# Recommender tower on one core: a segment's products and its table lookup issued alternately on TensorE, and ScalarE's copies reordered

## The reference, cut to what matters

```python
e = jnp.stack([tbl_0[ids[:, 0]], ..., tbl_25[ids[:, 25]]], axis=1)
combined = jnp.concatenate((dense_features[:, None, :], e), axis=1)      # 2048 x 27 x 128
interactions = jnp.einsum('bfd,bgd->bfg', combined, combined)
interactions_flat = interactions[:, iu, ju]                              # 351 pairs
h = jnp.concatenate([dense, interactions_flat, dense], axis=1)
h = jnp.maximum(h @ W_top1 + b_top1, 0.0)                                # 512
h = jnp.maximum(h @ W_top2 + b_top2, 0.0)                                # 256
y = h @ W_top3
```

## Time and profile before

| | |
|---|---|
| median of 3 runs | 406.02 us (405.79 to 406.1) |
| the profiled execution's own time | 405.83 us |
| its span, first to last instruction | 404.0 us |
| mean granted TensorE clock | 0.996 |
| TensorE matmul busy | 389.2 us (96%) |
| VectorE, ScalarE, GpSimd busy | 250.6, 221.8, 279.4 us |

### The profile page before, as it was taken

The page is one execution under the profiler, slowest core; times in us unless marked ns, Lnnn a source line. Parts: engine busy times, 40 slices in busy tenths (PEclk is TensorE's granted clock), DMA queues, the critical chain, the costliest instruction groups (busy, mean ns, idle before and its releaser), DMA issues.

```text
span 404.0 us, 8455 instructions
## 1 busy us (share of the span) xinstructions
PE 389.2 (96%) x3264; PEld 376.1 (93%) x3264; DVE 250.6 (62%) x683; ACT 221.8 (55%) x465; POOL 279.4 (69%) x296
## 2 busy tenths in 40 slices
PE   6978879999999999999999999999999999999998
PEld 4867779999999999999999999999999999999896
DVE  5899878568395737749375756739474765913421
ACT  2354177647464555737554664746455673756462
POOL 6777877777777777777777777777777777774000
PEclk9999989999999999999999999999999999999999
DMA  8996234323332332333333233333343222221000
GB/s 185 265 287 161 67 74 97 80 75 82 76 78 78 86 80 73 85 80 78 68 87 80 80 84 77 80 80 74 81 84 80 60 53 60 54 54 40 2 2 0
DMA packets 24596, 33.98 MB, mean 84 GB/s; under 512 B 8590, under 2 KB 18342, under 8 KB 24557
## 3 DMA queue, kind: packets, MB, share of 16 engines
q0 software_dynamic: 9216, 18.89, 19.4%
q1 hardware_dynamic: 13260, 14.41, 14.7%
q10 hardware_dynamic: 2080, 0.15, 0.5%
HBM read 33.41 MB, written 0.01 MB: 83 GB/s over the span
## 4 chain that ended last, share of the span: by engine, by line
PE 91%; DVE 4%; ACT 3%; issue 2%; DVEq 0%
PE look L511 29%; PE prod L541 26%; PE mlp L559 10%; PE turn L522 8%; PE mlp L570 6%; PE mlp L561 3%; PE mlp L506 3%; DVE onehot L400 2%; PE mlp L578 2%; PE prod L585 2%; ACT feats L293 1%; PE mlp L551 1%; ACT diag L308 1%; DVE table_lo L406 1%; PE prod L631 1%
## 5 line engine op out<-in xcount | busy, mean ns | idle before, releaser
L271 POOL DMA_INDIRECT rows<-in_tbl,ids x288 | 278.5, 967 | 89.2 <-issue 85.7
L308 ACT ACTIVATE diag<-prod 27x216 f32<-27x216 f32 x256 | 87.5, 342 | 139.8 <-PE prod L541 131.5
L400 DVE TENSOR_SCALAR onehot<-wanted,row_no 125x256 fp32r<-125x256 int32 x462 | 144.3, 383 | 13.1 <-PE look L511 13.1
L511 PE MATMUL look<-onehot,table_hi 125*128 125x256 f32 x494 | 128.3, 297 | 3.0 <-DVE onehot L400 2.7
L511 PE MATMUL look<-onehot,table_lo 125*128 125x256 f32 x494 | 123.1, 286 | 0.0
L541 PE MATMUL prod<-feats 128*123 128x108 f32 x1024 | 119.8, 270 | 2.2 <-ACT feats L293 2.2
L541 PEld LDWEIGHTS prod<-feats 128*123 128x123 f32 x1024 | 115.3, 188 | 3.2 <-ACT feats L293 3.0
L511 PEld LDWEIGHTS look<-onehot,table_hi 125*128 125x128 f32 x494 | 96.3, 195 | 4.3 <-issue 4.2
L428 DVE TENSOR_SCALAR h<-mlp,b_sb 128x128 f32<-128x128 f32 x86 | 24.9, 345 | 118.3 <-PE mlp L561 73.9
L511 PEld LDWEIGHTS look<-onehot,table_lo 125*128 125x128 f32 x494 | 96.6, 196 | 0.0
L293 ACT ACTIVATE feats<-turn 128x512 f32<-128x512 f32 (+1 forms) x80 | 78.3, 1019 | 1.1
(11 more groups left out here) (52 smaller groups left out, 145.8 us busy)
## 6 DMA issues: line engine op xcount, KB each, us to landing
wanted<-in_small_ids SPq DMA_DIRECT2D x56, 128.0 KB, 3.3
rows<-in_tbl,ids POOLq DMA_INDIRECT x288
feats<-in_tbl SPq DMA_DIRECT2D x7, 448.0 KB
dense<-in_dense_rows SPq DMA_DIRECT2D x16, 64.0 KB, 3.4
w_sb<-in_w_pairs SPq DMA_DIRECT2D x1, 702.0 KB
table<-in_tbl SPq DMA_DIRECT2D x1, 560.0 KB
w_sb<-in_w SPq DMA_DIRECT2D x1, 512.0 KB
feats<-in_tbl SPq DMA_DIRECT2D x7, 52.0 KB
```

What stands on the lines that cost most here:

```text
L271: gp.indirect_dma_start(rows[:, q % SLOTS_OF_ROWS, f * D:(f + 1) * D], None, large_tables[g + f], bass.IndirectOffsetOnAxis(ap=ids[:, t, g ...
L308: last = nc.scalar.activation(diag[t % 2][W * i:W * i + SLOTS, s * SEG_GROUPS * SLOTS:(s + 1) * SEG_GROUPS * SLOTS], prod_part(prod[s % 2] ...
L400: made = nc.vector.tensor_scalar(onehot[v % 2][:, c - row_nos_at(h), :], wants, row_no[:, c:c + 1], None, ALU.is_equal)
L511: last = nc.tensor.matmul(look_bank(v)[:, 0:BS], part_of(part, k)[:, c * D:(c + 1) * D], onehot[v % 2][:, c, :], start=(c == 0 and part is ...
```

## The change

In every segment that has a lookup, TensorE no longer does products and lookup one after the other. The new `products_and_look_up` first makes all waits of both, and then issues one group of the products, the two matmuls of one chunk of the lookup, the next group, and so on. The eighth table's last two chunks come at the end alone. `prod_full` is given by the eighth group, `look_full` by the last lookup matmul. The turned chunks and the tower parts follow behind. On ScalarE `empty_lookup` moves ahead of `empty_turn` and `place_dense`. The segments of tiles 14 and 15, the head and the other engines' orders stay.

```diff
                     if s == 0 and t >= 2:
                         copy_result(t - 2)
+                    if (v := lookup_at(t, s)) is not None:
+                        empty_lookup(v)
                     if t + 1 < TILES:
                         for k in TURNS_AT[s]:
                             empty_turn(t + 1, k)
                         if s == 1:
                             place_dense(t + 1)
-                    if (v := lookup_at(t, s)) is not None:
-                        empty_lookup(v)
...
-                if v >= NS:
-                    pe.wait_ge(look_read, v)
-                elif v >= 2:
+                if v >= 2:
                     pe.wait_ge(look_read, v - 1)
...
+            def products_and_look_up(t, s, v):
+
+                k = v % NS
+                wait_for_products(t, s)
+                if v < 2 * NS:
+                    pe.wait_ge(hi_ready[k], 1)
+                    pe.wait_ge(lo_ready[k], 1)
+                pe.wait_ge(onehot_ready, v + 1)
+                pe.wait_ge(look_read, v)
+                for c in range(CH[k]):
+                    if c < SEG_GROUPS:
+                        last_group = group_products(t, s, c)
+                        if c == SEG_GROUPS - 1:
+                            last_group.then_inc(prod_full, 1)
+                    for part in (table_hi, table_lo):
+                        last = nc.tensor.matmul(look[:, 0:BS], part_of(part, k)[:, c * D:(c + 1) * D],
+                                                onehot[v % 2][:, c, :], start=(c == 0 and part is table_hi),
+                                                stop=(c == CH[k] - 1 and part is table_lo))
+                last.then_inc(look_full, 1)
...
             for t in range(LAST):
                 for s in range(SEGS):
-                    products(t, s)
+                    if (v := lookup_at(t, s)) is not None:
+                        products_and_look_up(t, s, v)
+                    else:
+                        products(t, s)
                     if s == 0 and t >= 2:
                         third_layer(t - 2)
                     if t + 1 < TILES:
                         for k in TURNS_AT[s]:
                             turn_rows(t + 1, k)
-                    if (v := lookup_at(t, s)) is not None:
-                        look_up(v)
```

More of the change, by code:

```diff
@@ L495, in look_up @@
                     pe.wait_ge(raw_in[k], 32)
-                elif v == k or v == NS + k and k in WHOLE_FIRST:
+                else:
                     pe.wait_ge(hi_ready[k], 1)
@@ L524, in turn_rows, with wait_for_products @@
                 last.then_inc(turn_full, 1)
-            def products(t, s):
+            def wait_for_products(t, s):
                 m = SEGS * t + s
@@ L535, in products @@
                     pe.wait_ge(prod_read, m - 1)
-                for g in range(SEG_GROUPS):
[L537 to L543, removed]
@@ L544, in products, with group_products @@
-                last.then_inc(prod_full, 1)
+            def group_products(t, s, g):
+                at = t % FEAT_TILES * FT + (s * SEG_GROUPS + g) * P
+                own = feats[:, at:at + OWN]
+                group = feats[:, at:at + P]
+                to = (g // BANK_GROUPS) * BANK + (g % BANK_GROUPS) * GS * SLOTS
+                return nc.tensor.matmul(prod[s % 2][0:OWN, to:to + GS * SLOTS], own,
+                                        group.rearrange("d (s w) -> d s w", w=W)[:, :, 0:SLOTS],
+                                        start=True, stop=True)
@@ new lines, in products @@
+            def products(t, s):
+                wait_for_products(t, s)
+                for g in range(SEG_GROUPS):
+                    last = group_products(t, s, g)
+                last.then_inc(prod_full, 1)
+            def products_and_look_up(t, s, v):
+                k = v % NS
+                wait_for_products(t, s)
+                if v < 2 * NS:
[13 more added lines that the diff above has]
+                last.then_inc(look_full, 1)
```

## The result

The changed kernel takes 461.71 us (median of 4 runs, 460.75 to 461.89), the kernel before beside it 405.9: the ratio is 1.138, 95% interval 1.135 to 1.141. The profiled execution took 461.89 us with a span of 460.1, so 56.1 us more span.

What follows compares the result with a forecast made beforehand. TensorE's issue rate was taken to bound the kernel, busy 96% of the span; 405.83 us plus 46.5 for waits on ScalarE's copies in tiles 1 to 13 plus 8.0 in tile 0 gave 460, range 448 to 480.

Steps and rivals of the forecast that it cites:

- The pace of the weave: Woven segments on TensorE: a chunk of two product records and two lookup matmuls takes 0.457 us, bounds 0.435 and 0.467.
- 0.09 at each switch: Rival: every switch from products to lookup costs the third layer's 0.09 us, 40 us more, 500 us; chance 8%.
- quick weave: Rival: products and lookups hide parts of each other, chunk 0.34 us, kernel 408 us, paying for the waits; chance 5%.
- When ScalarE starts: Woven segment: ScalarE's products' copies start 3.61 us after the segment's start, where before it was 1.90.
- The segments: Steady tiles: segments 0 to 3 take 5.98, 5.81, 7.66 and 7.15 us; tile 26.60 against 23.02, 46.5 over thirteen tiles.
- 0.10 for a restart: TensorE's first products after a wait last 1.97 us and not 1.87, so 0.10 is lost in restarting.
- Tile 0: First tile: products also wait for VectorE's one-hot, TensorE stands some 5 us, tile 1 starts at 73.5, 8.0 us later.
- The sum: Whole kernel: 405.83 plus 46.5 for tiles 1 to 13 plus 8.0 for tile 0 gives 460.3 us.
- The signs: Expected in the trace: 39 TensorE waits of 0.4 to 1.5 us for ScalarE's copies in tiles 1 to 13, 40 to 45 us.
- The clock as a rival: Rival: stalls of 1.3 to 1.4 us cause a half-clock stretch per tile, 1.5 us each, 480 us; chance 8%.
- The estimate from the Trainium skill: Weights load while the present matmul streams: woven chunk 427.5 ns against 423, 2.0 us more over 448 chunks, nothing gained.
- The side remark: ScalarE's order: without the reordering, the turned chunk's copy, 1.14 us, would also stand in segments 0 and 1.

Runs made afterwards that it cites:

- e5: Changed kernel with ScalarE's products' (and result's) copies last in the segment, behind lookup's copy, turned chunks and dense copy; measured again as e5b: 415.98 us, ratio 1.025.
- e7: As e5, but tile 0 unwoven and in the old order on TensorE and ScalarE; second measurement 411.33 us, ratio 1.014.
- e2: Changed kernel with ScalarE's old order, the lookup's copy behind the turned chunk's; 516.1 us, ratio 1.275.
- e3: Kernel before, not woven, with only ScalarE's new order (lookup's copy moved ahead); 414.38 us, ratio 1.024.
- e6b: Changed kernel with only two of the four copies of the products in woven segments, for timing only; second measurement 431.87 us, ratio 1.065.
- e4: Changed kernel with waits still in front, but all eight product groups first, then all lookup chunks, not alternated; 423.66 us, ratio 1.046.
- e8b: Kernel before, not woven, with two pieces of VectorE's work put behind the main loop's first one-hot; second measurement 403.65 us, ratio 0.996.

## Why the prediction was right

The forecast was 460 us, measured 461.71, the profiled execution 461.89. Step by step:

- **The pace of the weave**, 0.457 a chunk: 0.455 in the trace (an eight-chunk weave with its third layer and turned chunk keeps the 4.74 us of before in e5). Product to lookup has no price of its own. The rivals that hung on it fell: no 0.09 at each switch (500 us), and no quick weave (408 us), since 0.455 leaves nothing of the 0.122 that it needed; e7 at 411 us shows no gain either once the waits are gone.
- **When ScalarE starts**, 3.61 into the segment: 3.68 and 3.65. The products' copies, the result's and the lookup's took their durations of before.
- **The segments**, 5.98, 5.81, 7.66, 7.15: they took 6.0, 5.82, 7.71, and 6.97 or 7.01. Segment 3 was forecast 0.15 too long, and segment 2 0.05 too short, because the 0.10 for a restart had been booked to the segment in front of the wait; it belongs to the one behind. In segments 0 and 1, which have a wait at either end, this cancels. In segment 3, which starts without a wait, ScalarE's copies begin 3.58 in, in the restarted ones 3.65 and 3.68. A tile came to 26.53, not 26.60: 1 us less over the run.
- **Tile 0**: tile 1 starts 8.9 us later, predicted 8.0. The stall was 4.79, near the 5 expected. About 0.5 of the 0.9 too little stood before the first product: tile 0 begins at 44.51 us instead of 44.03, ahead of all that is woven, and e5b, with TensorE's stream of the changed kernel, begins it at 44.03. The rest is the half-clock stretch, in which TensorE worked 4.3 us (53.63 to 57.9) instead of 3.0 (53.20 to 56.2).
- **What was not in the sum**: a second half-clock stretch at 75.0 to 78.4, behind the wait of 2.56, which adds about 1.5 us to tile 1. The clock had been treated as a matter of the steady tiles and tile 0 only.
- **The sum**: predicted 8.0 + 46.5 = 54.5. Measured 74.39 - 65.48 = 8.9 in tile 0, and 420.71 (tile 14's start) - 74.39 = 346.3 against 299.3, 47.0; together 55.9 of the 56.1 us of span. That the total is only 1.6 off is in part luck: 0.9 in tile 0 and 1.5 for the clock were missing, and the steady tiles were taken 1.0 too long.
- **The signs**: 39 waits in tiles 1 to 13, as forecast, but the view adds up 35.5 us of idle time for them and not 40 to 45; seven are shorter than 0.4 us (0.29 and 0.34) and one is 1.52. The view counts from the modelled end of a record, and records of 0.27 us start 0.11 apart where nothing waits, so each wait costs some 0.16 more than it lists (an estimate from these two numbers). The sign of a wrong forecast, a granted clock of 0.5 behind a stall of the tiles after tile 0, did come once, in tile 1.
- **VectorE** was never waited for by TensorE in tiles 1 to 13, and neither were the gathers.
- **The clock as a rival** was refuted for the change as made, but for tile 1: from 80 to 400 us it was granted whole with waits of 1.0 and 1.2 us in a row. It was confirmed for waits of 1.88 and 2.33 us in e2, at 1.6 us a fall, near the 1.5 that the rival had.
- **The estimate from the Trainium skill**, "TensorE: Matmul & The Clock Gate", on what happens when a matmul is issued, was that the mixture gains nothing. The trace agrees, 0.455 against 0.454, though the estimate's figures for the four (0.4275 and 0.423) lie some 6% under them. Its difference is nearer 1.9 us than 2.0 over the 448 chunks.

The side remark that without the reordering 1.14 more would stand in two segments was near for the waits, 0.9 and 1.1 more in the traces, and short for the whole: e2 is 54 us above the changed kernel, of which about 25 are those waits in tiles 2 to 13 (28.6 against 26.5), 20 the falls of the clock there, 8 tiles 0 and 1.

## What to carry to other kernels

Alternating two streams on TensorE ends both late: what waits for the first of them starts when the second is nearly done, and the work that hid its copying is gone. Before weaving, write down for each bank when its last matmul comes, what stands ahead of its copy in the copying engine's queue, and when TensorE wants it again. Where one copy releases what is wanted next and another what is wanted two segments later, the order of these two decides: here 46 of 56 us. An order has no merit by itself, though: the same move of the lookup's copy gave 54 us in the woven kernel and cost 9.6 in the kernel before (e3). No run gave the lookups a second bank, so whether the weave would cost nothing then stays open.

## What the runs showed of the hardware

- TensorE's clock and the waits of TensorE before it. Pairs of 1.0 and 1.2 us in each tile left it whole for 320 us; pairs of 1.88 and 2.33 us (e2) were followed by 13 falls to the half level in twelve tiles, and one tile had none. In tiles 0 and 1 of the kernels it fell behind waits of 1.83 (e6b), 2.02 (e3), 2.56, 2.71 and 4.79 us, and not behind 1.39 (e4, e5b) or 1.65 (e8b, and the head of the kernel before).
- One and the same kernel doesn't always have the fall: the 13 executions of the kernel before beside e8b split into six at a mean granted clock of 1.000 and seven at 0.996, 1.6 us apart in their medians. The traced execution, at 0.996, has the half-clock stretch of tile 0 and no other in its span, so that stretch is the likely difference; but the others were not traced.
- A wait costs something behind it too: the first lookup matmul of a woven segment comes 0.13 after the first product without a wait (e5b, segment 1), 0.21 after it behind a wait for the lookup's copy, 0.24 behind one for the turned chunks.
- Matmuls of two kinds, products of 108 columns on 123 weights in two records and lookup matmuls of 256 columns on 128 weights, pass from one to the other in either direction without loss: 0.455 us for the four, 0.454 as the sum of their separate paces.
